# A four-layer graph network on one core: the last layer's small matmuls on row and column groups of PE, and 24 sorted blocks of edges in place of 22

## The reference

```python
h = relu(layernorm(x)); x = x + gcn(h)                    # layer 0
h = relu(layernorm(x)); x = x + attention(h, src, dst)    # layer 1, four heads
h = relu(layernorm(x)); x = x + weighted(h, src, dst, w)  # layer 2, two steps
h = relu(layernorm(x))                                    # layer 3, the last layer
xw = h @ W
ew = edge_attr @ edge_w                                   # 16 -> 128, one row for each edge
out = segment_sum(xw[src] * ew, dst) + b
x = x + out
```

## Time and profile before

| | |
|---|---|
| time, median of 3 runs | 2854.08 us (2853.39 to 2858.77) |
| span of the profiled execution | 2789.0 us |
| PE busy | 2275.2 us (82%) |
| POOL busy | 1889.4 us (68%) |
| DVE busy | 1811.8 us (65%) |
| ACT busy | 1459.7 us (52%) |
| mean granted clock of PE | 0.924 |

### The profile page before, as it was taken

How to read it: one execution, slowest core, us unless ns; L and a number is a source line. 1 busy time by engine, 2 the same in 40 slices (tenths; PEclk the granted TensorE clock), 3 DMA queues, 4 the chain that set the end, 5 groups by cost and what they waited for, 6 DMA issues and landing times. The chain is left out here.

```text
span 2789.0 us, 65350 instructions
## 1 busy us (share of the span) xinstructions
PE 2275.2 (82%) x23024; PEld 1658.8 (59%) x23024; DVE 1811.8 (65%) x3137; ACT 1459.7 (52%) x2773; POOL 1889.4 (68%) x1286
## 2 busy tenths in 40 slices
PE   4577777774974888888888888778997999999998
PEld 3466666662432555555656566533544788888887
DVE  8799999994344776777777776411113666666665
ACT  0498989983025888888888887100002333223222
POOL 3487878831506877777787775277775787888884
PEclk7699999996985999999999999899997999999999
DMA  2366767666803111111111112898693332222223
GB/s 52 113 178 189 193 193 196 188 187 186 206 23 88 50 49 49 49 49 49 49 49 49 49 49 16 185 220 189 123 219 72 72 61 59 58 60 56 60 53 60
DMA packets 241964, 285.30 MB, mean 102 GB/s; under 512 B 162714, under 2 KB 180451, under 8 KB 238566
## 3 DMA queue, kind: packets, MB, share of 16 engines
q1 hardware_dynamic: 193035, 248.38, 36.0%
q0 software_dynamic: 48784, 35.00, 6.6%
HBM read 170.23 MB, written 112.10 MB: 101 GB/s over the span
## 5 line engine op out<-in xcount | busy, mean ns | idle before, releaser
L384 POOL DMA_INDIRECT scratch_slots<-sort_pay,sort_slot x440 | 638.8, 1452 | 201.3 <-issue 200.3
L1908 POOL TENSOR_TENSOR score<-score,rise 125x1000 f32<-125x1000 f32 x261 | 559.2, 2162 | 234.3 <-DVE peaks L1850 193.5
L2283 POOL DMA_INDIRECT gathered_rows<-scratch_projected,src_i x385 | 474.0, 1231 | 125.4 <-issue 116.8
L1850 DVE CUSTOM_DVE_ANT_0 score<-raw,log_in 125x1000 f32<-125x1000 f32 (+1 forms) x348 | 330.4, 969 | 177.4 <-PE raw L1707 104.5
L1727 PE MATMUL probsT<-ident,score 125*125 125x125 f32 x2175 | 352.2, 292 | 25.8 <-ACT score L1784 14.8
L1774 ACT ACTIVATE rise<-raw 125x1000 f32<-125x1000 f32 (+1 forms) x350 | 312.7, 918 | 114.0 <-PE raw L1707 75.9
L1727 PEld LDWEIGHTS probsT<-ident,score 125*125 125x125 f32 x2175 | 293.1, 198 | 104.4 <-DVE weighed L1864 56.7
L861 PE MATMUL built<-pair_weight,hot 125*128 125x125 bf16 x3750 | 247.1, 227 | 86.4 <-DVE pair_weight L806 85.1
L861 PEld LDWEIGHTS built<-pair_weight,hot 125*128 125x128 bf16 x3750 | 225.2, 103 | 103.4 <-DVE pair_weight L806 102.1
L1707 PE MATMUL raw<-QT,key 32*125 32x500 f32 x1200 | 182.7, 678 | 93.9 <-DVE peaks L1850 88.4
L1864 DVE COPY weighed<-probsT 125x500 f32<-125x500 f32 x400 | 250.0, 671 | 13.2 <-PE probsT L1727 12.7
(11 more groups left out here) (305 smaller groups left out, 4341.2 us busy)
## 6 DMA issues: line engine op xcount, KB each, us to landing
weights_in<-scratch_weightsT SPq DMA_DIRECT2D x50, 1093.8 KB
scratch_weightsT<-wT SPq DMA_DIRECT2D x25, 1367.2 KB
scratch_logs<-log SPq DMA_DIRECT2D x75, 437.5 KB
log_in<-scratch_logs SPq DMA_DIRECT2D x75, 437.5 KB
counts_in<-scratch_counts SPq DMA_DIRECT2D x25, 683.6 KB
scratch_counts<-cc SPq DMA_DIRECT2D x24, 683.6 KB
scratch_slots<-sort_pay,sort_slot POOLq DMA_INDIRECT x440
weights_in<-scratch_weightsT SPq DMA_DIRECT2D x50, 127.0 KB
```

Of the source, the lines that this page charges most:

```text
L384: nc.gpsimd.indirect_dma_start(rows, bass.IndirectOffsetOnAxis(ap=slot[:, c:c + 1], axis=0), pay[:, c, :], None).then_inc(sort["placed"][u ...
L1850: nc.vector.tensor_tensor_reduce(out=halves(score[u][h]), in0=seen, in1=halves(log_in[:]), scale=1.0, scalar=FLOOR, op0=ALU.add, op1=ALU.m ...
L1908: nc.gpsimd.tensor_tensor(score[u][h][:, here], score[u][h][:, here], rise[:, b, PIECE * (1 - k):PIECE * (2 - k)], ALU.add).then_inc(added, 1)
L2283: nc.gpsimd.indirect_dma_start(gathered[:, g % GATHERS, k, :], None, projected, bass.IndirectOffsetOnAxis(ap=src_i[:, FIRST + g, k:k + 1], ...
```

## The change

**In the last layer.** The mixing is four matmuls of 16 rows and 128 columns of output, one to a row group of PE (rows 0, 32, 64, 96), into four banks of `mixed_ps`, in place of two of 36 rows and 256. For it the slots lie 32 words apart in the buffer; one DMA loads a block, not two. The factors of an item are three matmuls on row groups (two of 32 rows and 256 outputs, one of 16 rows and 128), in place of two of 80 rows and 320, and have no banks of their own: they use the upper parts of the four banks of the mixing. `sum_edges` takes `hot`, 32 columns wide, as its weights, and the message as what streams: five matmuls of 128 outputs on four column groups. That leaves four partial sums; ACT copies them (`copy_parts`), one matmul with `fold` adds them (`fold_parts`), and DVE adds the result to `acc`. The sum comes a round after the factors and the fold a round after that. Since all of it shares the four banks, there are new waits on `s_copied`, `made`, `parted` and `added`.

**In the sort.** 24 blocks, not 22, so 168 rounds and 69 items. A batch is one block: 24 runs of 20 scatters, 11 of them in adjacency, 3 in layer 0, 10 in the weighted layers.

```diff
-BATCHES = 11
-PER_BATCH = 2
+BATCHES = 24
+PER_BATCH = 1
-SECOND_ROWS = 64
-SLOT_ROWS_TURNED = SECOND_ROWS + 2 * SLOT
+SLOT_ROWS = 32
+SLOT_ROWS_TURNED = 3 * SLOT_ROWS + SLOT
-PLACED_IN_ADJACENCY = 5
-PLACED_IN_FIRST_LAYER = 1
+PLACED_IN_ADJACENCY = 11
+PLACED_IN_FIRST_LAYER = 3
...
+                nc.vector.tensor_reduce(fold[:], ident[:].rearrange("p (j s) -> p s j", s=SPAN), axis=AX.X, op=ALU.add)
...
-            mixed_ps = e(nc.psum_tensor(unique("mixed_ps"), [FULL, 2, 512], F32))
+            mixed_ps = e(nc.psum_tensor(unique("mixed_ps"), [FULL, QUAD, 512], F32))
-            factor = e(nc.psum_tensor(unique("factor"), [FULL, 2, 512], F32))
-            HALF = EG * D // 2
-            sums = factor[:, 0, HALF:HALF + SPAN]
+            pair_factor = mixed_ps[0:P, 0:2, D:3 * D]
+            last_factor = mixed_ps[0:P, 2, D:2 * D]
+            part_sums = mixed_ps[:, 3, D:2 * D]
+            sums = mixed_ps[:, 3, 2 * D:2 * D + SPAN]
...
+                def copy_parts(g):
+                    act.wait_ge(reduced, g + 1)
+                    need(act, folded, g - 1)
+                    nc.scalar.copy(parts[:, g % 2, :], part_sums).then_inc(parted, 1)
...
                 def mix_attributes(r):
                     need(pe, s_copied, r)
-                    for half in range(2):
-                        rows = slice(half * SECOND_ROWS, half * SECOND_ROWS + 2 * SLOT)
-                        ins = nc.tensor.matmul(mixed_ps[:, half, 0:2 * D], pay_t[rows, r % 2, :],
-                                               quad_mix[rows].rearrange("r c d -> r (c d)"), start=True, stop=True)
+                    need(pe, made, items_factored[0])
+                    need(pe, parted, items_summed[0])
+                    need(pe, added, items_folded[0])
+                    for c in range(QUAD):
+                        rows = slice(c * SLOT_ROWS, c * SLOT_ROWS + EDIM)
+                        ins = nc.tensor.matmul(mixed_ps[:, c, 0:D], pay_t[rows, r % 2, :], quad_mix[rows], start=True, stop=True)
                     ins.then_inc(s_mixed, 1)
+                    rounds_mixed[0] = r + 1
...
                 def factors(g):
                     pe.wait_ge(kept, g + 1)
                     need(pe, made, g)
-                    need(pe, added, g)
+                    need(pe, s_copied, rounds_mixed[0])
                     for h in range(2):
-                        ins = nc.tensor.matmul(factor[0:P, h, 0:HALF], attrT[:, g % 2, :],
-                                               mix[:].rearrange("r c d -> r (c d)")[:, h * HALF:(h + 1) * HALF], start=True,
-                                               stop=True)
-                    ins.then_inc(factored, 1)
+                        rows = slice(2 * h * EDIM, 2 * (h + 1) * EDIM)
+                        nc.tensor.matmul(pair_factor[:, h, :], attrT[rows, g % 2, :],
+                                         mix[rows, 2 * h:2 * h + 2].rearrange("r c d -> r (c d)"), start=True, stop=True)
+                    rows = slice(4 * EDIM, 5 * EDIM)
+                    nc.tensor.matmul(last_factor, attrT[rows, g % 2, :], mix[rows, 4], start=True, stop=True).then_inc(factored, 1)
+                    items_factored[0] = g + 1
...
                 def sum_edges(g):
                     pe.wait_ge(made, g + 1)
                     pe.wait_ge(spotted, g + 1)
+                    need(pe, s_copied, rounds_mixed[0])
+                    need(pe, parted, g)
+                    need(pe, added, items_folded[0])
                     for k in range(EG):
-                        ins = nc.tensor.matmul(sums, message[:, g % 2, k, :], hot[:, g % 2, k, :], start=(k == 0),
-                                               stop=(k == EG - 1))
+                        at = k % 4 * SPAN
+                        ins = nc.tensor.matmul(part_sums[at:at + SPAN], hot[:, g % 2, k, :], message[:, g % 2, k, :],
+                                               start=(k < 4), stop=(k > 0))
                     ins.then_inc(reduced, 1)
...
+                def fold_parts(g):
+                    pe.wait_ge(parted, g + 1)
+                    need(pe, s_copied, rounds_mixed[0])
+                    need(pe, added, g)
+                    nc.tensor.matmul(sums, parts[:, g % 2, :], fold[:], start=True, stop=True).then_inc(folded, 1)
+                    items_folded[0] = g + 1
```

More of the change, by code:

```diff
@@ L1531, in fetch_last_layer @@
         sp.dma_start(last["mix"][k * EDIM:(k + 1) * EDIM, k, :], T["L3_gnn_edge_w"]).then_inc(last["in"], 16)
[L1532 to L1535 removed]
+    for k in range(4):
+        sp.dma_start(last["quad_mix"][k * SLOT_ROWS:k * SLOT_ROWS + EDIM, :], T["L3_gnn_edge_w"]).then_inc(last["in"], 16)
 LAST_LOADS = 3 + EG + 4 + 1
@@ L2462, in need @@
                     eng.wait_ge(sem, n)
-            def item_due(r):
-                g = item_of(r)
-                if r == ROUNDS:
-                    return ITEMS - 1
-                return g - 1 if g is not None and g >= 1 else None
             @block.sync
```

108 lines of the change are left out of this document (54 added, 54 removed).

## The result

The changed kernel takes 2920.03 us (median of 4 runs, 2904.47 to 2922.77), the kernel before beside it 2854.7 (4 runs): a ratio of 1.0207, 95% interval 1.0171 to 1.0243. The forecast was slower, 2884, with a range up to 2908. It is slower by 65 us. The direction was forecast, but by luck: the two terms that made the forecast slower, 60 us in earlier stages that rest on pauses of POOL, did not come, and the loss lies where the forecast had a gain.

What follows compares the result with a forecast made beforehand. It took PE to bound the last layer and POOL to end the weighted layers: 2854.1 - 32 (last layer) + 1.5 (sort) + 18 (adjacency) + 0 (layer 0) + 42 (weighted layers) = about 2884 us, range 2830 to 2908.

Steps and rivals of the forecast that it cites:

- the two terms that made the forecast slower: Stages before the last layer: adjacency +18 us and weighted layers +42 us, from POOL's waits at the ends of runs.
- What bounds the kernel: PE sets the last layer's pace (busy 596 of 602 us); POOL sets the weighted layers' end by some 2 us.
- Ends of runs: five more of 7.7, +38: Weighted layers: halved runs bring five more POOL waits of 7.7 us, +38 of the stage's +42.
- eleven in adjacency: Adjacency: eleven run ends of 6.5 us, 72 in all, put POOL's end near 687; the stage grows by 18 us.
- a wait for landing: Before a run's last scatter POOL waits until all earlier ones have landed: 2.3 us on idle DMA engines, 7 to 8 on busy.
- Rival (a): Earlier stages: the wait doesn't come with each run, so halved runs add none in all; 2828 to 2834 us, chance 0.20.
- Rival (b): Last layer: waits come as forecast, but mode changes and waits for ACT's copy eat PE's gain; 2916 us, chance 0.07.
- PE in the last layer: -32: Last layer: rounds of 2.53 us and items of 1.97 bring the loop from 602 to 570 us.
- way in and out: Last layer, PE: 0.18 us added to each set of matmuls running abreast, taken from attention's 0.15 to 0.20.
- the new wait: Last layer: factors, sum and fold wait for ACT's copy of the mixing; 0.05 us a round, from 0 to 0.25.
- Its worst case for the loop, +117: Last layer: no gain in the mixing, none abreast, a wait of 0.25; items of 3.13 us and rounds of 2.94.
- a lower clock: Last layer: a PE clock below 0.99 (0.92 in layer 0, where PE idles more) would take some of the gain.

Runs made afterwards that it cites:

- e3: The kernel before, unedited, single run beside the kernel before: 2796.5 us against 2795.4; rounds of 585 us in its profile.
- e12: The changed kernel, unedited, run again beside the kernel before: 2742.1 us against 2795.3, ratio 0.9822; rounds of 552 us.
- e4: The kernel before with 24 blocks in 8 batches, so runs of 60 scatters, single run: 2810.7 us against 2795.4.
- e5: The changed kernel, unedited, run again beside the kernel before: 2743.1 us against 2793.4, ratio 0.9807; rounds of 552 us.
- e16: The changed kernel, unedited, run once more beside the kernel before: 2744.4 us against 2795, ratio 0.9830.
- e14: The changed kernel with POOL's last-layer gathers replaced by plain loads that SP issues: 2743.1 us against 2852.5 for the kernel before, ratio 0.9615.
- e6: The kernel before with ACT's copy of the mixing made twice: 2922.4 us against 2917.0 for the kernel before, ratio 1.0024.
- e7: The changed kernel with ACT's copy of the mixing made twice: 3075.7 us against 2917.0 for the kernel before, ratio 1.0541.
- e15: The changed kernel with mixing and factors as before the change, in banks of their own: 2792.7 us against 2795.3 for the kernel before, ratio 0.9985.
- e18: The changed kernel with mixing and factors as before the change, own banks, run again: 2863.5 us against 2859.8 for the kernel before, ratio 1.0024.

## Why the prediction was wrong

**What bounds the kernel: half wrong.** That PE sets the last layer's pace held (e3: 583 of 587). That POOL is last in the weighted layers was read from 2 us in one trace. In e3 POOL's last scatter starts at 2124.6 and PE's last matmul of the stage ends at 2136.9. That the weighted layers go by DMA traffic is likely but not shown: 194 GB/s in the change for 182, and the last layer's first turning comes at 2166.8 for 2175.7 (e12 and e3: 2162.0 for 2181.2).

**"Ends of runs: five more of 7.7, +38", and eleven in adjacency: this is the step that failed.** It took a pause that stands before the last scatter of runs of 40 for one that belongs to a run's end. It belongs to the 40th scatter (e4), so runs of 20 have none. The reading as a wait for landing did not fit the rows of its own trace either. In adjacency, with a DMA share between 0.65 and 0.74 in each 50 us from 200 to 600, the pauses change from short to long and back:

```profile
307.49 2.21 POOL L384 DMA_INDIRECT scratch_slots<-sort_pay,sort_slot  x1 [2.39 <-issue]
...
405.76 1.37 POOL L384 DMA_INDIRECT scratch_slots<-sort_pay,sort_slot  x1 [8.05 <-issue]
...
497.70 2.04 POOL L384 DMA_INDIRECT scratch_slots<-sort_pay,sort_slot  x1 [2.58 <-issue]
```

Of the 60 us forecast for adjacency and the weighted layers there came +3.7 at SP's last stores (672.08 for 668.38, 2 of it the sort's), and by the first turning of the last layer it was -9 in all. Rival (a) said this, "if it goes by a number of scatters", with a chance of 0.20 and 2828 to 2834. By it the change would take 2795 - 32 + 1.5 + 4 (or 10) = 2769 to 2775 where nothing is late. It took 2742 to 2744. Between the spans of e12 and e3, 56.6 us apart, the stages ahead have -19, the rounds -33, and what lies behind the last turning -4.5; the medians beside each other are 50 to 53 apart.

**Rival (b), 2916, is the nearest number, and half of it is luck.** It had PE gain nothing, because changes of mode and waits for ACT's copy eat the gain. The waits for ACT's copy are indeed where the result's rounds lose. But it had the pauses' 60 us too, which did not come, and it had the price on every chip: where nothing is late PE gains its 33 us.

**PE in the last layer: -32, measured -33.** Where nothing is late the rounds went from 585 to 552. From the first turning to the last addition, which is nearer to the forecast's 602 and 570, it is 601.7 and 564.8 (the profile before, and e12), -37. By pieces: mixing to rows 0.44 (forecast 0.40 with its way in and out); factors 0.63 (0.83: all three run abreast, 2400.73 to 2401.36, the lower bound of 0.61); sum 0.53 (0.73, below its bound of 0.61); fold 0.31 (0.30); turning 0.14 (0.11). What that gained went into the new wait: the sum starts 0.93 us behind the rows' start, for 0.68 of work, so 0.25 a sum, and 0.14 before a fold alone, some 0.13 a round on average; the forecast had 0.05. In the rounds with a sum the wait was at the forecast's upper bound, and factors and sum were at or below their lower one, so the right total comes in part from errors that cancel. The way in and out as a term was right for the mixing, and too high for the sum. The rule of the Trainium skill (page "TensorEngine Tiling (Array Packing)", section "Key Properties") that a change of tiling mode drains the engine did not decide anything here; and the skill's 3.07 times (page "TensorE: Matmul & The Clock Gate", section "Measured speedup vs the span model") gave 0.28 for the mixing, where 0.44 stands from its first record to the rows'.

**The cost that no step had.** 178 us lie between the result and e12's time. The forecast bounded the wait for ACT's copy by ACT's own 586 ns, with an answer at once; in the profile that I had, the answers came at 0.31, at most 0.46. It asked "how long does the copy take" and not "what if the answer is late". Its worst case for the loop, +117 from waits of 0.25 and nothing abreast, was set aside for the rows of attention, where POOL issues no DMAs (none in the trace from 810 to 1772). And the sign was there to be seen: a profile 65 us under the median of its own kernel's runs says that the runs have something that the profile lacks. The forecast named a lower clock as a risk, and that came: stretches at the lower level followed waits of PE as the one shown, and the mean fell to 0.86.

**What is shown and what is argued.** Shown: the pause's place (e4), the rounds' saving without lateness (e5, e12, e16), that no result is late without POOL's indirect gathers (e14; two runs, and three of the kernel before), and that the change loses more by a late copy than the kernel before does (e6 with e7) and than the version with own banks (e15 with e18). Estimated: idle time (79) and clock (96) make up the 175 us of the rounds. Argued: that the clock falls because of the waits, and that among what e15 takes back it is the sharing that counts. Open: why results are late in some groups of runs only, and what holds them; and the kernel before has no profile from the result's own chip, so its rounds there, some 585 + 60 = 645 by its time, are an estimate.

## What to carry to other kernels

Compare a profile's span with the median before using its rows: here the 65 us of difference were the first trace of what decided the result. When two steps come to share a bank, the price is not the other engine's work but its answer time at its worst, so look for what makes answers late and count the waits inside a round. And before a pattern is extended to runs of another length, ask for the rows that tell "the last" from "the 40th"; if the trace has none, the two are rivals of equal rank.

## What the hardware showed that was not expected

- In some groups of runs and not in others ACT and DVE start up to 2.9 us after the matmul that they wait for (0.31 otherwise): in 49 of 168 rounds of the result's trace, in none of e12's. It is PE's semaphore update that is late; the reader follows it by 0.02 us. Where POOL issued nothing in the result's rounds the turning's answer took at most 0.48.
- POOL pauses before the 40th indirect scatter in a run, for 2.3 to 9.8 us, whether none or 20 follow, and a satisfied wait in between changes nothing; in runs of 20, and before gathers, there is no pause.
- The same program took 2743 in one group of runs and 2920 in another, 6.5% more; 175 of the 180 us between the two spans lie in one layer.
